# VectorE's tensor-scalar steps between SBUF tiles replaced in a fused cross-attention and mixture-attention kernel

## What is computed

```python
x = x + xattn(layernorm(x), ctx, lens)        # 16 heads, 77 keys with a length mask, then @ Wo
h = layernorm(x)
pooled = h.mean(axis=1)
hid = relu(pooled @ gw1.T + gb1)              # the gate
logits = hid @ gw2.T + gb2                    # top 2 of 8 experts, softmax over them
q, k, v = (svd_moe(h, p) for p in "qkv")      # h @ Wm.T plus the chosen experts' low-rank parts
x = x + svd_moe(softmax(q @ k.T) @ v, "o")    # 16 heads, 512 keys
# layernorm: (x - mean) / sqrt(var + eps)
```

## Time and profile before

| | |
|---|---|
| median of three runs (lowest, highest) | 1447.52 us (1447.41, 1452.75) |
| the profiled execution's own time | 1450.59 us |
| its span, first to last instruction | 1448.0 us |
| PE busy | 1387.6 us, 96% |
| DVE busy | 981.3 us, 68% |
| ACT busy | 905.1 us, 63% |
| POOL busy | 635.4 us, 44% |
| mean granted TensorE clock | 0.969 of full speed |

### The profile page before, as it was taken

One profiled execution on the slowest core, in us unless ns is written; L12 is line 12 of the kernel. 1 busy time (PEld: TensorE's weight loads), 2 busy tenths in 40 slices (PEclk: granted clock), 3 DMA queues, 4 the chain that ended last, 5 costly groups with the idle time before them and its releaser, 6 DMA issues.

```text
span 1448.0 us, 17119 instructions
## 1 busy us (share of the span) xinstructions
PE 1387.6 (96%) x5448; PEld 697.5 (48%) x5448; DVE 981.3 (68%) x1847; ACT 905.1 (63%) x1659; POOL 635.4 (44%) x355
## 2 busy tenths in 40 slices
PE   8888999999999999999999999999999999989987
PEld 5534544545545454455545454454545455444432
DVE  4534666777777676777778776776768777566562
ACT  2345564876648575776748665776749665575552
POOL 2001113554534444554625445462625545466665
PEclk9979998999999999999999999999999999999999
DMA  7242324332234224432245223432245223242310
GB/s 260 63 130 81 84 51 112 92 96 72 64 124 122 75 53 102 118 88 72 60 127 141 59 62 89 130 93 74 53 124 136 61 75 77 75 113 65 96 30 29
DMA packets 80816, 131.33 MB, mean 91 GB/s; under 512 B 27398, under 2 KB 34182, under 8 KB 77655
## 3 DMA queue, kind: packets, MB, share of 16 engines
q1 hardware_dynamic: 74007, 128.55, 32.9%
q10 hardware_dynamic: 6720, 1.70, 0.5%
HBM read 66.08 MB, written 12.21 MB: 54 GB/s over the span
## 4 chain that ended last, share of the span: by engine, by line
PE 74%; DVE 12%; ACT 7%; issue 3%; POOL 2%; DMA 1%; ACTq 1%; SPq 0%; DVEq 0%; POOLq 0%
PE pj L1312 39%; PE scT L1397 7%; PE acc L1418 6%; PE sc L1369 6%; PE sc L1358 2%; DVE negmax L1123 2%; PE pj L1427 2%; PE scT L1390 2%; PE pj L1406 2%; PE pj L1342 2%; DVE negmax L1167 1%; PE pj L1297 1%; ACT probs L1000 1%; ACT ks L953 1%; ACT xhat L870 1%
## 5 line engine op out<-in xcount | busy, mean ns | idle before, releaser
L1123 DVE TENSOR_REDUCE negmax<-sc 128x1 f32<-128x512 f32 x512 | 333.1, 682 | 132.1 <-PE sc L1369 130.8
L1000 ACT ACTIVATE probs<-scT 128x512 f32<-128x512 f32 x512 | 279.4, 593 | 198.3 <-PE scT L1397 162.1
L844 POOL TENSOR_TENSOR probs_sum<-probs_sum,probs 128x1024 f32<-128x1024 f32 x128 | 298.9, 2365 | 31.7 <-ACT probs L1000 31.6
L1312 PE MATMUL pj<-XT,Wqk 128*128 128x512 f32 x512 | 251.4, 598 | 1.1 <-DVE stage_lo L1099 1.0
L1369 PE MATMUL sc<-ks,qs 96*128 96x512 f32 x512 | 239.0, 519 | 6.2 <-DVE negmax L1123 2.4
L840 POOL TENSOR_TENSOR probs_sum<-probs 128x1024 f32<-128x1024 f32 x64 | 151.4, 2377 | 153.6 <-ACT probs L1000 153.0
L1397 PE MATMUL scT<-qs,ks 99*128 99x512 f32 x512 | 211.8, 482 | 5.7 <-ACT probs L1000 3.7
L850 POOL TENSOR_TENSOR uv_stack<-UVS_sb,uv_stack 96x1024 fp32r<-96x1024 f32 x32 | 75.7, 2366 | 208.5 <-ACT UVS_sb L892 208.5
L1397 PEld LDWEIGHTS scT<-qs,ks 99*128 99x128 f32 x512 | 92.5, 193 | 119.7 <-issue 60.0
L812 POOL TENSOR_TENSOR rstd<-vareps,minus_half 128x4 f32<-128x4 f32 x16 | 16.3, 1019 | 298.3 <-DVE minus_mean L1094 298.3
L1369 PEld LDWEIGHTS sc<-ks,qs 96*128 96x128 f32 x512 | 97.5, 193 | 95.0 <-DVE negmax L1123 41.7
(11 more groups left out here) (105 smaller groups left out, 1915.9 us busy)
## 6 DMA issues: line engine op xcount, KB each, us to landing
Wqk<-in_WmT SPq DMA_DIRECT2D x16, 1024.0 KB, 6.3
Wvo<-in_WmT SPq DMA_DIRECT2D x16, 1024.0 KB, 5.5
UVS_sb<-in_UVS SPq DMA_DIRECT2D x64, 192.8 KB, 3.1
qs<-stage_lo SPq DMA_DIRECT2D x136, 64.0 KB, 2.0
qs<-qs SPq DMA_DIRECT2D x34, 256.0 KB, 3.0
X<-in_x SPq DMA_DIRECT2D x8, 1024.0 KB, 8.5
ks<-stage_lo SPq DMA_DIRECT2D x128, 64.0 KB, 2.0
ks<-ks SPq DMA_DIRECT2D x32, 256.0 KB, 2.9
```

The lines of the kernel that those rows point to most:

```text
L844: nc.gpsimd.tensor_tensor(probs_sum[:, pair], probs_sum[:, pair], probs[:, kt % 2, pair], ALU.add)\
L1000: nc.scalar.activation(probs[:, kt % 2, jj, :], scT[:, ST[step], :], ACT.Exp, scale=SCALE)\
L1123: nc.vector.tensor_reduce(negmax[:, 0, n:n + 1], sc[:, SC[step], :], AX.X, ALU.max, negate=True)\
L1312: mm = nc.tensor.matmul(pj[:, p, :], lhsT, rhs, start=(dc == 0), stop=(dc == DC - 1))
```

## The change

Three DVE tensor-scalar steps that read SBUF and write SBUF are replaced. (1) ACT's logarithm is written straight into `negmax[:, 1]`, unscaled, and DVE's scaling (L1167) is gone; instead the two rows of `keys1` that meet the logarithm (99 and 100) hold -1/SCALE rather than 1, which takes two memsets on POOL in place of one. PE's transpose now waits for ACT. (2) The variance plus EPS becomes a DVE column sum over variance and a third column of `meanvar` that holds EPS; the negated mean becomes a DVE sum over one column with negation. (3) ACT's Relu writes the hidden column spread over 128 columns itself, and DVE's spreading step (L1202) is gone; PE waits for ACT. Steps on `consts_made` wait for 9 in place of 7, since POOL makes two more memsets. The calendar is the same.

```diff
-    nc.vector.tensor_scalar(vareps[:], meanvar[:, :, 1], EPS, None, ALU.add)
-    nc.vector.tensor_scalar(minus_mean[:], meanvar[:, :, 0], -1.0, None, ALU.mult)
+    dve.wait_ge("consts_made", 3)
...
+    nc.vector.tensor_reduce(vareps[:], meanvar[:, :, 1:3], AX.X, ALU.add)
+    nc.vector.tensor_reduce(minus_mean[:], meanvar[:, :, 0:1], AX.X, ALU.add, negate=True)
...
 def cln(step, b, i):                       # ScalarE
-    act.wait_ge("cross_scaled", act.after("cross_scaled", "cln", *before))
+    act.wait_ge("pj_full", act.after("pj_full", "cross_shift", *before))
     act.wait_ge("cross_summed", act.after("cross_summed", "csum", b, i, TT - 1))
-    nc.scalar.activation(cross_sums[:], cross_sums[:], ACT.Ln)
+    nc.scalar.activation(negmax[:, 1, HJ * TT:2 * HJ * TT], cross_sums[:], ACT.Ln)
...
-def cln(step, b, i):                       # VectorE
...
-    nc.vector.tensor_scalar(negmax[:, 1, HJ * TT:2 * HJ * TT], cross_sums[:], -1.0 / SCALE, None, ALU.mult)
...
 def gate_hidden(step, b):                  # ScalarE
-    nc.scalar.activation(hidden[:], pj[:, PJ[step], 0:1], ACT.Relu, bias=gb1_sb[:], scale=1.0 / S)
+    nc.scalar.activation(hiddenB, pj[:, PJ[step], 0:1].to_broadcast([P, P]), ACT.Relu, bias=gb1_sb[:], scale=1.0 / S)
...
-def gate_hidden(step, b):                  # VectorE
...
-    nc.vector.tensor_scalar(hiddenB, ident_sb[:], 0.0, hidden[:, 0:1], ALU.mult, ALU.add)
...
 # GpSimd's memsets
+    (meanvar[:, :, 2:3], EPS)
-    (keys1[MASK_ROW:CROSS_ROWS, :, :, :].bitcast(F32), 1.0),
+    (keys1[MASK_ROW:CROSS_ROWS, :, :, :].bitcast(F32), -1.0 / SCALE),
+    (keys1[MASK_ROW:LN_ROW, :, :, :].bitcast(F32), 1.0),
...
 # TensorE
-    turned(step, 1, "cross_scaled", ("cln", b, i))
+    turned(step, 1, "cross_ln", ("cln", b, i))
-    pe.wait_ge("gate_step", pe.after("gate_step", "gate_hidden", b))
+    pe.wait_ge("pj_left_by_act", pe.after("pj_left_by_act", "gate_hidden", b))
```

More of the change, by code:

```diff
@@ L29 @@
 ROWS = SHIFT_ROW + 2
+LN_ROW = SHIFT_ROW + 2
 CROSS_ROWS = SHIFT_ROW + 4
@@ L410, in increments @@
     if kind == "cln":
-        return {"cross_ln": 1, "cross_scaled": 1}
+        return {"cross_ln": 1}
     if kind == "cacc":
@@ L424, in increments @@
     if kind == "gate_hidden":
-        return {"pj_full": 1, "pj_left_by_act": 1, "gate_step": 1}
+        return {"pj_full": 1, "pj_left_by_act": 1}
     if kind == "gate_top":
@@ L596, in cross_and_mixture_attention @@
         bn = sb("bn", [P, TT, 6])
-        meanvar = sb("meanvar", [P, TT, 2])
+        meanvar = sb("meanvar", [P, TT, 3])
         vareps = sb("vareps", [P, TT])
@@ L603, in cross_and_mixture_attention @@
         pooled = sb("pooled", [P, DC])
-        hidden = sb("hidden", [P, 1])
         hiddenB = xhat[:, 0, 0:P]
@@ L700, in context @@
                 sp.wait_ge("mask_stored", 16)
-                sp.wait_ge("consts_made", 7)
+                sp.wait_ge("consts_made", 9)
                 sp.wait_ge("scoresT_full", sp.after("scoresT_full", "csT", b - 1, DC - 1, HJ - 1))
@@ L800, in _ @@
             for n, (what, value) in enumerate((
-                    (negmax[:], 0.0), (minus_half[:], -0.5), (K1[:, :, :, NK:NKP], 0.0), (ones[:], 1.0),
-                    (keys1[MASK_ROW:CROSS_ROWS, :, :, :].bitcast(F32), 1.0),
+                    (negmax[:], 0.0), (minus_half[:], -0.5), (meanvar[:, :, 2:3], EPS), (K1[:, :, :, NK:NKP], 0.0), (ones[:], 1.0),
+                    (keys1[MASK_ROW:CROSS_ROWS, :, :, :].bitcast(F32), -1.0 / SCALE),
+                    (keys1[MASK_ROW:LN_ROW, :, :, :].bitcast(F32), 1.0),
                     (qsc[MASK_ROW:MASK_ROW + 1, :, :].bitcast(F32), 1.0),
@@ L895, in split_keys @@
                 act.wait_ge("pj_left_by_dve", act.after("pj_left_by_dve", "context_keys", DC - 1, half))
-                act.wait_ge("consts_made", 7)
+                act.wait_ge("consts_made", 9)
                 nc.scalar.activation(K1_hi[:, :, 4 * half:4 * half + 4, :], K1[:, :, 4 * half:4 * half + 4, :], ACT.Copy)\
@@ L979, in cln @@
                 before = (b, i - 1) if i else (b - 1, DC - 1)
-                act.wait_ge("cross_scaled", act.after("cross_scaled", "cln", *before))
+                act.wait_ge("pj_full", act.after("pj_full", "cross_shift", *before))
                 act.wait_ge("cross_summed", act.after("cross_summed", "csum", b, i, TT - 1))
-                nc.scalar.activation(cross_sums[:], cross_sums[:], ACT.Ln).then_inc(sems["cross_ln"], 1)
+                nc.scalar.activation(negmax[:, 1, HJ * TT:2 * HJ * TT], cross_sums[:], ACT.Ln).then_inc(sems["cross_ln"], 1)
             def csT(step, b, i, j):
@@ L1014, in gate_hidden @@
                 act.wait_ge("pj_full", act.after("pj_full", *step))
-                nc.scalar.activation(hidden[:], pj[:, PJ[step], 0:1], ACT.Relu, bias=gb1_sb[:], scale=1.0 / S)\
+                nc.scalar.activation(hiddenB, pj[:, PJ[step], 0:1].to_broadcast([P, P]), ACT.Relu, bias=gb1_sb[:], scale=1.0 / S)\
                     .then_inc(sems["pj_left_by_act"], 1)
@@ L1090, in deviation @@
                 for t in range(TT):
-                    nc.vector.bn_aggr(meanvar[:, t, :], bn[:, t, :]).then_inc(sems["ln_step"], 1)
+                    nc.vector.bn_aggr(meanvar[:, t, 0:2], bn[:, t, :]).then_inc(sems["ln_step"], 1)
+                dve.wait_ge("consts_made", 3)
                 dve.wait_ge("ln_step", dve.after("ln_step", *step, k=TT))
-                nc.vector.tensor_scalar(vareps[:], meanvar[:, :, 1], EPS, None, ALU.add).then_inc(sems["ln_step"], 1)
-                nc.vector.tensor_scalar(minus_mean[:], meanvar[:, :, 0], -1.0, None, ALU.mult).then_inc(sems["ln_step"], 1)
+                nc.vector.tensor_reduce(vareps[:], meanvar[:, :, 1:3], AX.X, ALU.add).then_inc(sems["ln_step"], 1)
+                nc.vector.tensor_reduce(minus_mean[:], meanvar[:, :, 0:1], AX.X, ALU.add, negate=True).then_inc(sems["ln_step"], 1)
             def q1_split(step, b, i):
@@ L1111, in csc @@
                 before = (b, i - 1) if i else (b - 1, DC - 1)
-                dve.wait_ge("consts_made", 7)
+                dve.wait_ge("consts_made", 9)
                 dve.wait_ge("pj_full", dve.after("pj_full", "cross_shift", *before))
@@ L1157, in csum @@
                 before = (b, i - 1) if i else (b - 1, DC - 1)
-                dve.wait_ge("cross_scaled", dve.after("cross_scaled", "cln", *before))
+                dve.wait_ge("cross_ln", dve.after("cross_ln", "cln", *before))
                 dve.wait_ge("cross_exped", dve.after("cross_exped", "cexp", b, i, t))
@@ L1161, in csum @@
                                         AX.X, ALU.add).then_inc(sems["cross_summed"], 1)
-            def cln(step, b, i):
[L1164 to L1168, removed]
             def inv(step, b, j, part):
@@ L1198, in token_sums @@
                     nc.vector.tensor_reduce(pooled[:], tile_sums[:], AX.X, ALU.add).then_inc(sems["gate_step"], 1)
-            def gate_hidden(step, b):
-                dve.wait_ge("pj_left_by_act", dve.after("pj_left_by_act", *step))
-                nc.vector.tensor_scalar(hiddenB, ident_sb[:], 0.0, hidden[:, 0:1], ALU.mult, ALU.add)\
-                    .then_inc(sems["gate_step"], 1)
             def gate_top(step, b):
@@ L1253, in _ @@
                       "qk_split": qk_split, "csc": csc, "sc": scores, "shift": turn, "cross_shift": cross_turn,
-                      "cless": cless, "csum": csum, "cln": cln, "inv": inv, "residual1": residual1, "residual2": residual2,
-                      "token_sums": token_sums, "gate_hidden": gate_hidden, "gate_top": gate_top,
+                      "cless": cless, "csum": csum, "inv": inv, "residual1": residual1, "residual2": residual2,
+                      "token_sums": token_sums, "gate_top": gate_top,
                       "gate_scale": gate_scale, "weff": weff, "v_bias": v_bias})
@@ L1351, in csc @@
                 if t == 0:
-                    pe.wait_ge("consts_made", 7)
+                    pe.wait_ge("consts_made", 9)
                     pe.wait_ge("keys1_loaded", pe.after("keys1_loaded", "context", b))
```

## The result

The changed kernel takes 1427.08 us (median of four runs, 1425.31 to 1428.46) against 1447.91: a ratio of 0.985, 95% interval 0.982 to 0.987. Its profiled execution took 1427.25 us with a span of 1425.1.

The account below looks back on a forecast made before the run. PE, busy 96% of the span, was taken to bound the kernel through its waits and clock falls. From the profiled 1450.59 us, 20.5 (six steady batches) + 2 (gate) + 1.2 (first batch) = 23.7 us gave 1427; range 1416.3 less 2 us, to 1440.

Parts of the forecast that it names:

- What bounds: Whole kernel: PE is busy 96% of the span, so only what idles or slows PE can move the end.
- The wait for GpSimd: DVE's SBUF-to-SBUF tensor-scalars wait until POOL has an end between two instructions; L1167 176 ns median, 2471 at most.
- Part (1): Logarithm's scaling in steady batches: removing it ends two PE waits and the clock falls, 165.21 to 162.18 us a batch.
- The clock's share: Steady batches: without the gaps the clock stays full, so a batch takes 163.70 us against 165.21 on average.
- The share of the gaps: Steady batches: PE's waits of 0.84 us at the transpose and 0.68 behind it go, 163.70 to 162.18 us.
- Parts (2) and (3): Layer norm sums end PE's 0.38 us wait for `pooled` each steady batch; the gate's spreading step gone gives 2 us overall.
- Part (4): First batch: half of 2.3 us of PE waits for L1167 and L1202 goes, 1.2 us; bounds 0 and 2.3.
- The end of the run: Sixth steady batch: counted with the same full gain as the others, 3.41 us, six batches giving 20.5 us.
- The wait that only moves: Rival, steady batches: PE waits as long for the next late thing, likely POOL; about 1447 us, chance 0.14.
- Stalling sums: Rival, layer norm: sums reading SBUF also wait for POOL, costing 2.3 us of the gain; 1429 us, chance 0.06.
- A fall of the clock that grew: Rival, steady batches: one gap becomes several small ones with a long clock fall; 1470 us, chance 0.04.

Follow-up runs that it names:

- bystanders: Changed kernel plus one VectorE instruction nobody reads: tensor-scalar at the logarithm 1445.4 us (4 columns 1444.0), at the gate 1427.0; as a sum at the logarithm 1426.2.
- the run with halved sums: Kernel before, with each of GpSimd's sums of probabilities cut into two instructions of half the length: 1501.7 us in one run.
- the run with the logarithm alone: Kernel before, with only ScalarE writing the logarithm into its rows, VectorE's scaling gone and key rows scaled: 1428.1 us against 1448.9, ratio 0.988.

## Why the prediction was right, point by point

**What bounds.** Right. What PE loses by idling and by a slow clock was the price that counted: 41 us of DVE's busy time went and 22.9 us of span. The bystanders show it most plainly: one instruction costs 19 us at the logarithm, with six long stalls, and nothing that one run shows at the gate, with six of about 1.6 us.

**The wait for GpSimd.** Right that the tensor-scalar form waits and the sum doesn't (1431.4 and 1426.2 us with sums in its place, 1445.4 with an unread tensor-scalar). This is the exclusive lock of the Trainium skill's page SBUF — State Buffer, "SBUF: two separate sides", as far as who waits; the traces agree. They compare the form of the step: that the two-port mode of the form is what takes the lock is what that page of the Trainium skill says, and no run here takes mode and form apart. Wrong in one sentence: "waits on DVE until POOL has an end between two of its instructions". The row under it already showed L1167 passing the end of L850 at 802.84, and in the run with halved sums it passed several. The sum of the prediction didn't rest on it, since it took the stall's price from PE's waits.

**Part (1).** The price of a batch was to fall from 165.21 to 162.18; alone it fell to 161.55. The clock's share, 1.51, came out as reckoned, since no fall was left between 250 and 1240 us. The two windows in which the prediction compares "what PE did before" the clock fell or stayed hold the stall itself, and the second one already the fall (0.80), so they don't show what came before it. The share of the gaps was 163.70 - 161.55 = 2.15 us where the two visible waits are 1.52, so this term was too small by 0.6 us a batch. PE's idle time in the records fell by 1.7 us (2.4 to 0.7); where the rest came from, gaps that PE's modelled ends hide or something else, is not shown.

**Parts (2) and (3).** They were put at 0.38 + 2 / 6 = 0.7 us a batch; the change has 161.55 - 160.91 = 0.64 on top of part (1). For `vareps` the step is right: 161 ns against 170 reckoned, the 0.38 us wait for `pooled` gone, 2.4 us alone (0.6 to 4.3) against 2.3. For the gate the 2 us are not shown: alone it is 2.4 with an interval that holds zero, and a 1.6 us stall put back at its place into the changed kernel costs nothing in one run. The Relu takes 371 ns, not 343; PE waits for it once, 0.6 us.

**Part (4).** Not found. 1.2 us were to come in the first batch, and its end is 0.8 us later. But the same kernel, run again, has its mark at 261.04 in place of 262.25, and the run with the logarithm alone has it at 258.58. Differences of this size in the start are scatter.

**The end of the run.** The sum gave the sixth batch its full 3.4 us; from the last mark on only 2.2 came. The clock lost more behind the end of the sixth batch, as windows of 40 us show that start 173.2 us behind the last mark of each kernel (before, then after):

```profile
1260.72:1300.72 40.00, 35.86 (x132) 17.50 (x131) 28.52 (x53) 27.94 (x50) 23.06 (x11) 0.91 0.40 107
```

```profile
1240.00:1280.00 40.00, 36.30 (x128) 17.45 (x127) 26.03 (x45) 27.75 (x49) 22.13 (x11) 0.87 0.42 110
```

That is 40 x 0.04 = 1.6 us more of full-speed clock lost; at the prediction's 2.64 / 3.4 = 0.78 it is an estimated 1.2 us, as much as is missing.

**The total.** It is right in part because two errors met: each of the five batches gained 4.3 us where parts (1) to (3) had 3.7, and the start and the stretch from the last mark on gained less than their terms. The size of the change also hangs on where one starts. The sum took 23.7 us off the profiled execution's 1450.59; profile to profile the kernel lost 23.3, but median to median 20.8. That the forecast should start from the profiled execution, since it had more falls of the clock than the median one, was argued in the prediction, and the 13 runs of before on one chip bear it out: the fastest (1444.97 us) has a mean clock of 0.975, the slowest (1454.14 us) one of 0.966.

**The rivals.** The wait that only moves did not come: PE is idle for 2.3 of 990 us, with POOL as busy as before. Stalling sums did not come: no sum of this change spreads by more than a few ns. A fall of the clock that grew came only behind the sixth batch, and small.

## What to carry to other kernels

Read a line's minimum, median and maximum before its mean: a small VectorE instruction that is 176 ns at the median and 2471 at most is waiting inside, and the timeline of the other engines says for whom. Where GpSimd runs long instructions, write small SBUF-to-SBUF steps of VectorE as sums, or give them to ScalarE or to a constant operand. Price such a stall by what TensorE waits for behind it in VectorE's queue, with what the clock loses after the gap, not by its length or by who reads its result.

## What the runs showed of the hardware that was not expected

A tensor-scalar on VectorE can be passed over at the ends of several GpSimd instructions that follow each other closely: one took 8.37 us, past the ends of L852, of L822 and of four halves, where another, at another place, was served at the next end (1.05 us). What decides between the two was not found; the size of its tile does not (up to 2524 ns with 4 columns, 2527 with 16). Halving GpSimd's sums lengthened that wait from 2.3 to 8.4 us, and the kernel took 54 us more in the one run.
